# Message stage of a relational graph layer: the slot kinds move to VectorE, the coefficients become four long GpSimd passes

## The reference, cut to what matters

```python
# 3125 nodes, 103125 edges sorted by dst, 8 relations, 4 bases, 128 features
Hb   = jnp.einsum('ni,bio->bno', h, V)
coef = w_comp[etype]                                   # (edges, 4)
m    = sum(coef[:, b][:, None] * Hb[b][src] for b in range(4)) * norm[:, None]
agg  = jax.ops.segment_sum(m, dst, num_segments=n_nodes)
hn   = jax.nn.relu(agg + h @ loop_w + bias)
y    = hn @ ffn_w.T + ffn_b + h
x1   = layernorm(x + layernorm(y) * ln_g + ln_b)       # first layer
x2   = layernorm(x1 + two_graph_attention_layers(x1))  # second, two heads of 64
```

## Time and profile before

| | |
|---|---|
| median of 3 runs | 2381.31 us (2379.43 to 2386.92) |
| the profiled execution | 2376.36 us, its span 2374.6 us |
| message stage | about 1140 us of the span |
| PE busy, 160 to 1120 us | 935.10 of 960 us |
| DVE busy there | 787.48 us |
| POOL busy there | 681.67 us |
| one step (one tile), mean of 22 | 44.36 us |

### The profile page before, as it was taken

The page is one execution under the profiler, slowest core; times in us unless marked ns, Lnnn a source line. Parts: engine busy times, 40 slices in busy tenths (PEclk is TensorE's granted clock), DMA queues, the critical chain, the costliest instruction groups (busy, mean ns, idle before and its releaser), DMA issues. The chain is left out here.

```text
span 2374.6 us, 55414 instructions
## 1 busy us (share of the span) xinstructions
PE 2223.8 (94%) x19740; PEld 1726.4 (73%) x19740; DVE 1575.0 (66%) x4047; ACT 1296.4 (55%) x2317; POOL 833.0 (35%) x1091
## 2 busy tenths in 40 slices
PE   1399999999999999999979999999999999999998
PEld 0388889888888888888855666666665566666666
DVE  2468878878878878877734655655651666666665
ACT  1166666566566566566634555555552455555555
POOL 0857767767767767767200000000000000000000
PEclk9599999999999999999989999999997999999999
DMA  4011111111111111111121211222201222222220
GB/s 114 13 38 41 48 49 41 44 53 41 46 50 41 48 49 41 48 50 38 42 93 55 82 68 67 81 81 81 81 27 56 85 69 80 87 87 87 87 87 7
DMA packets 52282, 141.44 MB, mean 60 GB/s; under 512 B 9253, under 2 KB 43499, under 8 KB 45599
## 3 DMA queue, kind: packets, MB, share of 16 engines
q1 hardware_dynamic: 49548, 129.42, 15.3%
q0 software_dynamic: 2576, 9.68, 1.5%
HBM read 93.82 MB, written 45.27 MB: 59 GB/s over the span
## 5 line engine op out<-in xcount | busy, mean ns | idle before, releaser
L776 PE MATMUL ps<-matrixT,x_rows 125*128 125x256 f32 (+1 forms) x2500 | 581.6, 383 | 2.8 <-ACT aggT L862 2.1
L1524 DVE CUSTOM_DVE_ANT_0 scores_l<-ps,bias_rows_l 125x500 f32<-125x500 f32 (+1 forms) x700 | 406.8, 620 | 214.9 <-issue 209.3
L843 ACT COPY matrixT<-ps 125x500 f32<-125x500 f32 (+2 forms) x800 | 395.8, 584 | 223.8 <-PE ps L764 221.2
L776 PEld LDWEIGHTS ps<-matrixT,x_rows 125*128 125x128 f32 x2500 | 459.8, 190 | 71.2 <-issue 3.0
L1453 ACT COPY weightsT_l<-ps 125x500 f32<-125x500 f32 (+1 forms) x450 | 238.0, 540 | 448.3 <-PE ps L1391 445.7
L1391 PEld LDWEIGHTS ps<-eye,scores_l 125*125 125x125 f32 x2500 | 307.3, 188 | 214.1 <-issue 146.9
L764 PE MATMUL ps<-high_weights,low_onehot 64*125 64x125 f32 x6300 | 404.6, 279 | 23.6 <-issue 11.5
L764 PEld LDWEIGHTS ps<-high_weights,low_onehot 64*125 64x125 f32 x6300 | 367.0, 189 | 53.4 <-issue 31.3
L1391 PE MATMUL ps<-eye,scores_l 125*125 125x125 f32 x2500 | 387.4, 291 | 7.0 <-ACT scores_l L1432 6.8
L1367 PE MATMUL ps<-kT_l,q_tile_l 64*125 64x500 f32 (+1 forms) x1400 | 358.8, 591 | 5.0 <-DVE chunk_max_l L1524 3.9
L1354 PE MATMUL ps<-weightsT_l,values_l 125*64 125x125 f32 x5000 | 345.7, 277 | 0.0
(11 more groups left out here) (156 smaller groups left out, 1959.2 us busy)
## 6 DMA issues: line engine op xcount, KB each, us to landing
bias_rows_l<-bias SPq DMA_DIRECT2D x50, 1562.5 KB, 6.6
bias<-bias SPq DMA_DIRECT2D x150, 250.0 KB, 2.0
edges<-rec POOLq DMA_DIRECT2D x1, 2014.2 KB, 11.8
x_rows<-in_x SPq DMA_DIRECT2D x1, 1562.5 KB
bias<-bias SPq DMA_DIRECT2D x25, 62.5 KB, 1.6
x<-x_rows SPq DMA_DIRECT2D x25, 62.5 KB
x_rows_l<-x SPq DMA_DIRECT2D x25, 62.5 KB
out<-rows_l SPq DMA_DIRECT2D x25, 62.5 KB
```

Source lines behind the costliest of these rows:

```text
L776: last = nc.tensor.matmul(psG[:, BASES * SPLIT * side:BASES * (SPLIT * side + SIDE[side])], x[:, h, :], MT[side][:, 0:SIDE[side], BASES * ...
L843: last = nc.scalar.copy(MT[side][:, at:at + 2 * c - 1:2, 0:COLS], psP[bank][0:R, :].rearrange("p (i c) -> p i c", c=128)[:, 0:c, 0:COLS])
L1524: V.tensor_tensor_reduce(S[par][:, hd, lo:hi], psS[2 * ((par + j) % 2) + hd][0:R, 0:cw[j]], bias[par][0:R, lo:hi], 1.0, FLOOR, ALU.add, AL ...
```

## The change

- DVE gets a new part, `slot_kinds(t-1)`, as the last work of its period k = 7: one comparison for the empty slots (`own_slots`), eight instructions of 128x64 that make the kinds times the weight in one go each, and the two digit planes, an addition and a copy. It waits for the slots of the DMA, for the first pass of the POOL part of the tile before (`mixed`), and signals `kinds_ok`.
- `coefs(t-2)` on POOL has only four instructions left: the product of the kinds with `w_comp` for all four bases at once (128x2048), and three additions by halves (128x4x256, 128x4x128, 128x256). `coef_parts` is four times as large.
- On POOL `coefs` stands between the two powers of `root`; before, it stood behind both and behind `lift`. `third` on DVE, which wants the second power, moves from k = 1 to k = 4.
- `find_slots` also waits for `kinds_ok` of two tiles before. PE turns the codes at k = 4 and no longer at k = 5, and ACT copies them out at k = 4.

```diff
             def coefs(s, par):
-                then(nc.gpsimd.tensor_copy(node_p[:, :], ids[:, bass.ds(s, 1)]))
-                pool.wait_ge(ell_in[par], (half(s, par) + 1) * 16)
...
-                for r in range(RELS):
-                    last = nc.gpsimd.tensor_scalar(kinds[:, r, :], e[:, 2, :], float(r), None, ALU.is_equal)
-                then(last)
-                then(nc.gpsimd.tensor_tensor(kinds[:, :, :], kinds[:, :, :], e[:, 3:4, :].to_broadcast([128, RELS, SLOTS]), ALU.mult))
-                for b in range(BASES):
...
+                pool.wait_ge(kinds_ok, s + 1)
+                nc.gpsimd.tensor_tensor(part[:, :, :, :], kinds[:, :, :].unsqueeze(1).to_broadcast([128, BASES, RELS, SLOTS]), c,
+                                        ALU.mult).then_inc(mixed, 1)
+                pool.wait_ge(mixed, s + 1)
+                then(nc.gpsimd.tensor_tensor(part[:, :, 0:4, :], part[:, :, 0:4, :], part[:, :, 4:8, :], ALU.add))
+                then(nc.gpsimd.tensor_tensor(part[:, :, 0:2, :], part[:, :, 0:2, :], part[:, :, 2:4, :], ALU.add))
                 if not is_int(s) or s >= 2:
                     pool.wait_ge(codes_ps, s - 1)
...
+                nc.gpsimd.tensor_tensor(to[:, 2:PLANES, :], part[:, :, 0, :], part[:, :, 1, :], ALU.add).then_inc(codes_ok, 1)
...
             def step(t, par):
                 if inside(t - 5):
                     root(t - 5, 1 - par, 0)
+                if inside(t - 2):
+                    coefs(t - 2, par)
+                if inside(t - 5):
                     root(t - 5, 1 - par, 1)
                 if inside(t - 4):
                     lift(t - 4, par)
-                if inside(t - 2):
-                    coefs(t - 2, par)
...
+            def slot_kinds(s, par):
+
+                then = Steps(v, s3, s)
+                e = ell[par].rearrange("p (s c) -> p c s", c=FIELDS)
+                v.wait_ge(ell_in[par], (half(s, par) + 1) * 16)
+                then(V.tensor_scalar(off[:, :], e[:, 4, :], node[par][:, :], OWN, ALU.is_equal, ALU.mult))
+                if not is_int(s) or s >= 1:
+                    v.wait_ge(mixed, s)
+                for r in range(RELS):
+                    V.scalar_tensor_tensor(kinds[:, r, :], e[:, 2, :], float(r), e[:, 3, :], ALU.is_equal, ALU.mult)
+                if not is_int(s) or s >= 2:
+                    v.wait_ge(codes_ps, s - 1)
+                V.tensor_tensor(codes[par][:, 0, :], e[:, 0, :], off[:, :], ALU.add)
+                V.tensor_copy(codes[par][:, 1, :], e[:, 1, :]).then_inc(kinds_ok, 1)
...
-                    if k == 1 and inside(z):
+                    if k == 4 and inside(z):
                         third(z, 1 - par)
...
+                    if k == PERIODS - 1 and inside(t - 1):
+                        slot_kinds(t - 1, 1 - par)
...
-                    if k == 5 and inside(w + 1):
+                    if k == 4 and inside(w + 1):
                         turn_codes(w + 1, par)
```

More of the change, by code:

```diff
@@ L41 @@
 AFTER, LEAD = 5, 7
-COEF_STEPS = 19
+COEF_STEPS = 2
 OWN = 512.0
@@ L452, in message @@
         ell = [sb(f"slots{i}", [128, SLOTS * FIELDS], F32) for i in range(2)]
-        node_p = sb("node_p", [128, 1], F32)
         off = sb("own_slots", [128, SLOTS], F32)
         kinds = sb("kinds", [128, RELS, SLOTS], F32)
-        part = sb("coef_parts", [128, RELS, SLOTS], F32)
+        part = sb("coef_parts", [128, BASES, RELS, SLOTS], F32)
         codes = [sb(f"codes{i}", [128, PLANES, SLOTS], F32) for i in range(2)]
@@ L488, in message @@
          ctA_ok, ctB_ok, c_ps, ln_ok, masked, bias_ok, xt_ok, m_ps, hrow_ok, h_ps, h_ok, y_ps, y_ok, x_ok, x_ps, x_t_ok, asked1, rooted1,
-         asked2, rooted2, nrm1, nrm2, lifted) = (
+         asked2, rooted2, nrm1, nrm2, lifted, s3, kinds_ok, mixed) = (
             sem("m_" + n) for n in (
@@ L493, in message @@
                 "hrow_ok", "h_ps", "h_ok", "y_ps", "y_ok", "x_ok", "x_ps", "x_t_ok", "asked1", "rooted1", "asked2", "rooted2",
-                "norms1", "norms2", "lifted"))
+                "norms1", "norms2", "lifted", "s3", "kinds_ok", "mixed"))
         row_in = [sem("row_in0"), sem("row_in1")]
@@ L530, in coefs @@
                 then = Steps(pool, gps, s * COEF_STEPS)
-                e = ell[par].rearrange("p (s c) -> p c s", c=FIELDS)
                 to = codes[par]
-                then(nc.gpsimd.tensor_copy(node_p[:, :], ids[:, bass.ds(s, 1)]))
-                pool.wait_ge(ell_in[par], (half(s, par) + 1) * 16)
-                hold(2, s)
-                then(nc.gpsimd.tensor_scalar(off[:, :], e[:, 4, :], node_p[:, :], OWN, ALU.is_equal, ALU.mult))
+                c = comp[:, :].rearrange("p (r b) -> p b r", b=BASES).unsqueeze(3).to_broadcast([128, BASES, RELS, SLOTS])
@@ L537, in coefs @@
                 if not is_int(s) or s >= 2:
                     pool.wait_ge(codes_ps, s - 1)
-                nc.gpsimd.tensor_tensor(to[:, 0, :], e[:, 0, :], off[:, :], ALU.add)
-                nc.gpsimd.tensor_copy(to[:, 1, :], e[:, 1, :])
-                for r in range(RELS):
-                    last = nc.gpsimd.tensor_scalar(kinds[:, r, :], e[:, 2, :], float(r), None, ALU.is_equal)
-                then(last)
-                then(nc.gpsimd.tensor_tensor(kinds[:, :, :], kinds[:, :, :], e[:, 3:4, :].to_broadcast([128, RELS, SLOTS]), ALU.mult))
@@ L553, in coefs @@
-                last.then_inc(codes_ok, 1)
+                nc.gpsimd.tensor_tensor(to[:, 2:PLANES, :], part[:, :, 0, :], part[:, :, 1, :], ALU.add).then_inc(codes_ok, 1)
                 pool.wait_ge(codes_ok, s + 1)
@@ L565, in find_slots @@
             def find_slots(s, par):
+                if not is_int(s) or s >= 2:
+                    pool.wait_ge(kinds_ok, s - 1)
                 pool.wait_ge(slot_ok, s + 1)
```

## The result

The changed kernel takes 2452.89 us (median of four runs, 2449.02 to 2462.5), the kernel before 2382.97 beside it (four runs, 2379.43 to 2386.92). The ratio is 1.0312, with a 95% interval of 1.0273 to 1.0351. It is slower, as forecast, and by 25 us more than the forecast of 2428 us, inside the range. The profiled execution is the longest of the four, 2462.5 us with a span of 2460.8.

A forecast was written before the change was run, and what follows sets the result against it. The prediction took PE to bound the kernel and, after the change, to wait for a late DVE group: 22 steps of 2.44 us more, 54 us, less 7 at the start, gave 2428 us, range 2388 to 2475.

The forecast's parts named there:

- The path and its place: Long POOL passes block DVE's build for k = 0, so PE waits for `high_weights` at k = 2, 2 to 4 us.
- The layout of the seam: Start times on DVE and POOL after `first`: DVE blocked 6.5 us, group ready at T0 + 15.5 against T0 + 11.9.
- T0: The end of `first` on DVE, from which the forecast counts each step; POOL starts its first power 0.09 us later.
- The step: PE's step as group time after T0 plus 31.3 us: 46.8 us, 2.44 more than 44.36, over 22 steps.
- the 31.3 us: PE's own work from taking the group at k = 2 to the next T0, without its wait for POOL.
- The start: Start of the stage: first codes reach PE at about 78 us, a gain taken as 7 us.
- The sum: 22 steps of 2.44 us more, 54 us, less 7 at the start: +47 us, 2428 us.
- The store of x1: `third` at k = 4 puts this store ahead of two bias stores on SP; unhidden, a few tenths a step.
- The one in which PE stays the bound: Rival: long passes give way to DVE, group ready at T0 + 9.0, 20 us faster, 2361 us; 14 in 100.
- The one in which gains and waits cancel: Rival: short kinds, L703 and L704 not blocked, group ready near T0 + 13.4, time within 0.3%; 6 in 100.
- The one for slower by more: Rival: first pass 4.5 us and kinds 3.2, +88 us, 2469; or x1 store holds PE, 22 us; 15 in 100.

The follow-up runs named there:

- e2: The changed kernel with its four long POOL passes cut into sixteen short ones, still between the two powers; 2403.29 us, ratio 1.0113.
- e3: The changed kernel with sixteen short POOL passes at the old place behind `lift` and `third` back at k = 1; 2359.88 us, ratio 0.993.
- e4: The changed kernel with the first three POOL passes left out, one single-element instruction in their place; 2349.91 us, ratio 0.9862.
- e8: e3 with `third` at k = 4 in place of k = 1; 2381.52 us, ratio 1.004.
- e11: The kernel before with `third` moved from k = 1 to k = 4 and nothing else; 2396.3 us, ratio 1.0075.
- e5: The changed kernel with `third` back at k = 1; 2455.15 us, ratio 1.0313.
- e7b: e3 with nine useless one-input DVE instructions ahead of the group of k = 0; 2451.29 us, ratio 1.0333.
- e1: The changed kernel with its four long POOL passes back behind both powers and `lift`; 2436.48 us, ratio 1.0244.

## Why the prediction was right, and short by 25 us

**The path and its place: right.** PE waits at the pair products of k = 2 for `high_weights`, 61.8 us over 21 places, and e2, e3 and e4 take this wait away by taking the long passes away.

**The layout of the seam: right to 0.1 us.** K, when DVE is through with the kinds, was put at T0 + 4.4; it is 560.72 + 0.22 = T0 + 4.42. The passes were 3.67, 2.31, 1.23 and 0.71; they are 3.68, 2.35, 1.27 and 0.73. The group was to be ready at T0 + 15.5; it is at 571.97, T0 + 15.45. L708 and L709, the old L703 and L704, are blocked too, 2.51 and 1.31 us in place of the 0.35 of the earlier trace rows.

The Trainium skill (SBUF — State Buffer, Who interferes with whom) has the two engines lock each other out for whole instructions where DVE reads two SBUF inputs; the trace agrees, with the rows above, also for the SCALAR_TENSOR_TENSORs that no row of before showed. The Trainium skill's price of 4497 ns for 2048 elements (GPSIMD Engine Reference, 3.1 Elementwise) differs from the measurement of the first pass, 3.68 us, and the measurement decides. The additions, whose two inputs are both full, lie on 0.19 us + 2.1 ns an element (2.35, 1.27 and 0.73 us); for 2048 elements that would be 4.5 us, an estimate. So the page's price fits the additions; the product, of which one input is a broadcast, is cheaper, and no run here shows whether that is why.

**The step: the idle part was right, the clock was missing.** PE's idle time a step was (1 - 0.9742) x 44.36 = 1.14 us in the kernel before (974.22 us busy of 1000) and is (1 - 0.9257) x 48.32 = 3.59 us (925.66 of 1000). That is 2.45 more, where the sum had 2.44. But PE's busy time a step rose from 43.2 to 44.7 us for the same matmuls. The term that was too small is the second in "the whole step becomes (the time of the group after T0) + 31.3 us": the 31.3 us were read from a step at clock 1.00, and behind its wait PE runs at the lower clock, which costs it 1.5 us, in some steps twice. Over 22 steps, 22 x (48.32 - 46.8) = 33 us are missing in the forecast. The steady stretch of before (160 to 1120 us) has no such wait, its longest on PE being 1.5 us, and it stood at clock 1.00; I had nothing in the sum for what a longer one does. The trace of before did have the price, at the start of the stage, where the granted clock was 0.50 (timeline and columns of the kernel before):

```profile
85.00:95.00 10.00, 5.28 (x56) 4.83 (x56) 6.77 (x9) 1.10 (x4) 8.32 (x11) 0.50 0.12 32
90.66 3.73 PE L764 MATMUL ps<-high_weights,low_onehot 64*125 64x125 f32 x32 [3.23 <-DVE high_weights L662]
```

**The start: more than forecast.** PE gets the first codes at 77.83 us, as forecast (78); on ACT the third tile's are 12.2 us earlier than before (155.42 against 167.62), where I had taken 7.

**The sum.** At the last copy of codes the changed kernel is 1218.40 - 1143.62 = 74.8 us behind: 22 x 3.96 = 87.1 less 12.2. What comes behind it is the same code in both; from the last copy of codes to the end of the span it took from 1222 to 1256 us in the profiled executions of the fourteen kernels, so its share in the difference of two single executions (1242.4 - 1231.0 = 11.4 us) says nothing. The medians differ by 70 us, where the forecast had 47: 33 more by the clock, 5 less by the start, and 5 less that a single profiled execution cannot place.

**The store of x1: hidden, but larger than I said.** I gave "a few tenths a step unhidden"; in kernels in which DVE is in time it is 1.1 to 1.2 us a step (e8, e11), about 1.0 of it idle time of PE in e8 and half of it in e11, where the rest came with the clock. In the changed kernel it is covered (e5).

**The rivals.** The one in which PE stays the bound, 2361 us, needed a long pass that gives way to DVE in the middle; L680 stood still for the whole of it. The one in which gains and waits cancel needed L703 and L704 not blocked; they were. The time of the first came out only in another kernel: 2355 to 2360 us with short passes at the old place and `third` where it was. The one for slower by more had a longer first pass and longer kinds, or the x1 store on top. The kinds took 2.18 us (558.76 to 560.94), the pass 3.68, and the store was hidden; what made the time longer, the clock, none of them named.

What stays open: why PE's clock falls behind some waits of about 2 to 3 us and not behind others like them. It fell in 18 of the 22 steps of the changed kernel, with waits of 1.8 to 3.6 us, in 7 of e7b, with waits of 1.2 to 2.9, and in e11 behind six of eight waits of 2.2 to 2.3.

## What to carry to other kernels

Where VectorE and GpSimd both read two inputs from SBUF, weigh the length of each GpSimd instruction and not their sum: a VectorE instruction that meets one loses up to its whole length (3.7, 2.3 and 1.2 us here for three that had taken 0.3). Four long passes did the work of sixteen in 8.0 instead of 10.2 us and cost 50 us of the kernel at the new place (the changed kernel against e2) and 55 at the old one (e1 against e8). Lay out the seam by start times before merging instructions, and ask of each instruction moved in program order which wait on its own engine, and which DMA queue, it now stands in front of. When the forecast has the bound TensorE waiting for some two microseconds or more at a time, as it did here, add to the sum what the matmuls behind the wait take at the lower clock.

## What the runs showed of the hardware

- VectorE and GpSimd take turns by whole instructions. L680, 0.29 us long by itself, ended 0.14 us after the pass that held it (561.17 + 3.67 against 561.02 + 3.68), L708 and L709, 0.35 us by themselves, 0.15 us after theirs. Neither held the other where the DVE instruction had one input: nine of them between 801.35 and 806.50 us in e7b took 0.53 to 0.55 us each, and POOL's first four short passes beside them 1.05, 0.73, 0.45 and 0.32.
- After a wait of 1.8 to 3.6 us in a stretch otherwise full, TensorE often fell from 2.4 to 1.2 GHz for one or two groups of matmuls: 3.6 in place of 2.01 us for 32 matmuls, granted clock 0.69 to 0.83 over 10 us. It did so behind all 14 waits of 3.3 to 3.6 us of the changed kernel and behind 4 of its 8 shorter ones. In the profiled executions of e2, e3, e4 and e8, whose waits were under 1.7 us, it stayed at 1.00 over the 1000 us. It fell in kernels without long passes as well (e7b, e11).
